# Two attention stages with a new order of steps on every engine, double buffers for probabilities and queries, the fp16 copy on GpSimd and the row normalisation on ScalarE

## The reference

```python
x = x + tanh(g_xattn[0]) * L0_xattn(layernorm(x), ctx, ...)   # q, k, v with bias, then an MLP 256-512-256
x = x + tanh(g_ffn[0])   * L0_ffn(layernorm(x), ...)          # 4-bit blocks, 704 wide
x = x + tanh(g_xattn[1]) * L1_xattn(layernorm(x), ctx, ...)   # masked, then @ Wo
x = x + tanh(g_ffn[1])   * L1_ffn(layernorm(x), ...)          # top 2 of 8 experts

# the core of both attentions, 16 heads of 16
q = (x @ Wq + bq).reshape(B, N, 16, 16)
scores = einsum('bnhd,bmhd->bhnm', q, k) * scale
attn = softmax(scores, axis=-1)
out = einsum('bhnm,bmhd->bnhd', attn, v).reshape(B, N, 256)
```

## Time and profile before

| | us |
|---|---|
| median of 3 runs | 799.55 |
| lowest, highest | 798.21, 802.42 |
| the profiled execution | 796.8 |
| its span | 795.0 |

### The profile page before, as it was taken

The page is one execution under the profiler, slowest core; times in us unless marked ns, Lnnn a source line. Parts: engine busy times, 40 slices in busy tenths (PEclk is TensorE's granted clock), DMA queues, the critical chain, the costliest instruction groups (busy, mean ns, idle before and its releaser), DMA issues.

```text
span 795.0 us, 16679 instructions
## 1 busy us (share of the span) xinstructions
PE 606.7 (76%) x5555; PEld 534.3 (67%) x5555; DVE 565.0 (71%) x1205; ACT 368.3 (46%) x905; POOL 205.8 (26%) x185
## 2 busy tenths in 40 slices
PE   4547787879934588888896599999874599999960
PEld 3237677769933377777785488888764389999950
DVE  5956766757898689999985367878747695455437
ACT  2335656563214444444443246565635355555530
POOL 3434243350020000000001133342500366555530
PEclk9999999999975599999998799999965599999995
DMA  7010000003000000000000000000059212222219
GB/s 219 1 60 1 2 2 2 2 2 110 0 1 0 0 1 0 0 0 0 0 1 1 0 2 2 2 2 2 2 177 381 73 48 80 75 81 78 77 50 307
DMA packets 27626, 36.62 MB, mean 46 GB/s; under 512 B 4024, under 2 KB 22265, under 8 KB 27438
## 3 DMA queue, kind: packets, MB, share of 16 engines
q1 hardware_dynamic: 23822, 25.56, 9.9%
q0 software_dynamic: 3744, 10.23, 4.2%
HBM read 26.47 MB, written 9.31 MB: 45 GB/s over the span
## 4 chain that ended last, share of the span: by engine, by line
PE 33%; DVE 22%; issue 6%; ACT 2%; DMA 1%; DVEq 1%; POOL 0%; SPq 0%; ACTq 0%; POOLq 0%
PE ps L1358 8%; PE ps L1359 7%; PE ps L1360 7%; PE ps L1459 3%; PE ps L1742 2%; DVE fhs L696 2%; DVE fh L754 2%; DVE x_sb L940 2%; DVE fha L705 1%; DVE fha L704 1%; PE ps L1684 1%; PE ps L1428 1%; DVE el_w L817 1%; PE ps L1678 1%; PE ps L1719 1%
## 5 line engine op out<-in xcount | busy, mean ns | idle before, releaser
L989 POOL TENSOR_TENSOR p_lo<-prob,p_hi 128x616 f16<-128x616 f32 x64 | 87.4, 1365 | 165.9 <-ACT prob L1100 162.4
L970 POOL TENSOR_TENSOR rstd<-mv,eps_col 128x16 f32<-128x16 f32 (+2 forms) x6 | 1.3, 209 | 272.7 <-DVE mv L471 272.7
L1108 ACT ACTIVATE pT<-ps 128x512 f32<-128x512 f32 (+1 forms) x96 | 50.7, 533 | 40.8 <-PE ps L1444 40.7
L577 DVE TENSOR_REDUCE smax<-ps 128x8 f32<-128x616 f32 x64 | 50.8, 794 | 19.0 <-PE ps L1360 12.8
L582 DVE TENSOR_TENSOR prob<-ps,smax 128x308 f32<-128x308 f32 x128 | 55.3, 474 | 7.3 <-POOL p_lo L989 3.0
L1358 PE MATMUL ps<-kbd_hi,q_hi 128*128 128x308 f32 x128 | 50.7, 396 | 10.7 <-DVE q_lo L566 9.3
L1032 POOL DMA_INDIRECT y_rows<-rn,dst_row x39 | 43.1, 1106 | 54.6 <-DVE rn L919 53.4
L460 DVE CAST ehT_hi<-ehid 128x512 fp32r<-128x512 f32 x39 | 16.7, 428 | 52.9 <-ACT ehid L1335 52.9
L1459 PE MATMUL ps<-vbd_flat,pT 128*128 128x34 bf16 (+1 forms) x1600 | 47.2, 183 | 6.0 <-ACT pT L1108 4.7
L1028 POOL DMA_INDIRECT xin<-x_rows,src_row x39 | 38.2, 979 | 52.5 <-DVE dst_row L886 40.9
L1099 ACT ACTIVATE p_hi<-prob 128x616 f16<-128x616 f32 x64 | 46.9, 733 | 9.6 <-DVE prob L582 9.4
(11 more groups left out here) (280 smaller groups left out, 2034.1 us busy)
## 6 DMA issues: line engine op xcount, KB each, us to landing
el_w<-in_L_ffn_W_dram SPq DMA_DIRECT2D x16, 512.0 KB, 9.8
eh_w<-y_rows SPq DMA_DIRECT2D x16, 256.0 KB, 6.2
x_sb<-in_x_dram SPq DMA_DIRECT2D x4, 512.0 KB, 8.6
x_rows<-rn SPq DMA_DIRECT2D x4, 512.0 KB, 10.0
out_dram<-x_sb SPq DMA_DIRECT2D x16, 128.0 KB, 4.5
stage<-in_L_xattn_W_dram SPq DMA_DIRECT2D x2, 512.0 KB, 3.7
eb<-in_L_ffn_b_dram SPq DMA_DIRECT2D x1, 1024.0 KB, 9.4
w<-in_L_ffn_w_down_dram SPq DMA_DIRECT2D x1, 704.0 KB, 7.6
```

Of the source, the lines that this page charges most:

```text
L577: ch.link(dve.tensor_reduce(top.rearrange("p (b h) -> p b h", h=HPB), sc, AX.X, ALU.max))
L989: pool.tensor_tensor(p_lo[:, c], prob[:, c], p_hi[:, c], ALU.subtract).then_inc(s["lo"], 1)
L1108: act.activation(dst, ps[:, 4 + g % 2, 0:(c[g + 1] - c[g]) * P // 2], ACT.Copy).then_inc(s["pev"], 1)
```

## The change

- `normalise` moves from VectorE to ScalarE, as an activation with scale `rstd` and bias `shift_a` = -mean x rstd. GpSimd makes `shift_a` (`shift_rows`, two small operations) before the barrier in front of each attention.
- `exp` is done once, in single precision, in place. `p_hi` is now a copy with conversion on GpSimd (`high_half`), followed by the difference (`low_half`), in the order low(t-1, second half), high(t, first), low(t, first), high(t, second).
- `prob`, `p_hi`, `p_lo`, `q_hi`, `q_lo` have two buffers, by the parity of the tile or pair.
- Each engine's `step(k)` gives every operation a distance in tiles. TensorE: query of k+2, x transposes of k+3, o transposes of k-2, scores of k+1, p transposes 1 and 2 of k-1, project of k-2, values of k-1, p transpose 0 of k. VectorE: residual of k-3, xT_lo of k+2, shift and norm, o_low of k-2, moments of k-3, q_lo of k+2. ScalarE: normalise k+4, first exponential, copies, xT_hi of k+3, q_hi of k+2, second exponential last. All steps are written out, and no engine has a loop in these stages.

The core of the diff:

```diff
-                def exp(t, h):
-                    if h == 0:
-                        att_wait(act, n, "lo", 2 * t)
-                        att_wait(act, n, "pt", 3 * t)
+                def exp(t, par, h):
                     att_wait(act, n, "shifted", 2 * t + h + 1)
                     c = slice(h * HM // 2, (h + 1) * HM // 2)
-                    act.activation(p_hi[:, c], prob[:, c], ACT.Exp).then_inc(s["hi"], 1)
-                    act.activation(prob[:, c], prob[:, c], ACT.Exp).then_inc(s["exp"], 1)
+                    act.activation(prob[:, par, c], prob[:, par, c], ACT.Exp).then_inc(s["exp"], 1)
...
+                def normalise(p):
+                    att_wait(act, n, "xt", p)
+                    for k in range(2):
+                        t = 2 * p + k
+                        ins = act.activation(xn[:, k], x_sb[:, t], ACT.Identity, bias=shift_a[:, n, bass.ds(t, 1)],
+                                             scale=rstd[:, 2 * n, bass.ds(t, 1)])
+                    ins.then_inc(s["xn"], 1)
...
+            def shift_rows(k, n, part):
+                pool.wait_ge(rs[n], part)
+                ch.link(pool.tensor_tensor(shift_a[:, k], mv[:, n, :, 0], rstd[:, n], ALU.mult))
+                pool.tensor_scalar(shift_a[:, k], shift_a[:, k], -1.0, None, ALU.mult).then_inc(rs[n], 1)
...
+            def high_half(n, t, h):
+                att_wait(pool, n, "exp", 2 * t + h + 1)
+                if h == 0:
+                    att_wait(pool, n, "pt", 3 * (t - 1))
+                c = slice(h * HM // 2, (h + 1) * HM // 2)
+                pool.tensor_copy(p_hi[:, t % 2, c], prob[:, t % 2, c]).then_inc(s["hi"], 1)
+            def both_halves(n):
+                for t in range(TILES):
+                    if t:
+                        low_half(n, t - 1, 1)
+                    high_half(n, t, 0)
+                    low_half(n, t, 0)
+                    high_half(n, t, 1)
+                low_half(n, TILES - 1, 1)
...
-                    att_wait(dve, n, "lo", 2 * (t - 1) + h + 1)
+                    att_wait(dve, n, "lo", 2 * (t - 2) + h + 1)
...
-                    att_wait(act, n, "scores", 4 * p)
+                    att_wait(act, n, "scores", 4 * (p - 1))
```

The new step of TensorE and of ScalarE:

```diff
+                def step(k):
+                    t, soon, now = k, k + 3, k + 2
+                    if 0 <= now < TILES and now % 2 == 0:
+                        query(now // 2)
+                    if 0 <= soon < TILES and soon % 2 == 0:
+                        x_transpose(soon // 2)
+                    if 0 <= t - 2 < TILES:
+                        o_transpose(t - 2)
+                    if 0 <= t + 1 < TILES:
+                        scores(t + 1, 0)
+                    if 0 <= t - 1 < TILES:
+                        p_transpose(t - 1, 1)
+                        p_transpose(t - 1, 2)
+                    if 0 <= t - 2 < TILES and n:
+                        project(t - 2)
+                    if 0 <= t + 1 < TILES:
+                        scores(t + 1, 1)
+                    if 0 <= t - 1 < TILES:
+                        values(t - 1)
+                    if 0 <= t < TILES:
+                        p_transpose(t, 0)
...
+                def step(k):
+                    t, later, soon, now = k, k + 4, k + 3, k + 2
+                    if 0 <= later < TILES and later % 2 == 0:
+                        normalise(later // 2)
+                    if 0 <= t < TILES:
+                        exp(t, t % 2, 0)
+                    if 0 <= t - 1 < TILES:
+                        p_out(t - 1, 0)
+                    if 0 <= soon < TILES and soon % 2 == 0:
+                        x_high(soon // 2)
+                    if 0 <= t - 2 < TILES:
+                        o_high(t - 2)
+                    if 0 <= now < TILES and now % 2 == 0:
+                        q_high(now // 2, now // 2 % 2)
+                    if 0 <= t - 1 < TILES:
+                        p_out(t - 1, 1)
+                        p_out(t - 1, 2)
+                    if 0 <= t < TILES:
+                        exp(t, t % 2, 1)
```

186 lines of the change are left out of this document (59 added, 127 removed).

## The result

| | before | after |
|---|---|---|
| median, us | 798.88 | 753.68 |
| lowest, highest | 798.06, 802.42 | 752.68, 754.52 |
| the profiled execution | 796.8 | 754.5 |
| its span | 795.0 | 752.8 |

The ratio of the medians is 0.9426, with a 95% interval of 0.9394 to 0.9457: 45 us faster, where 34 were forecast. The time lies 3.3 us under the lower end of the range.

What follows compares the result with a forecast made beforehand. TensorE was taken to bound both attentions. Gains of 7.7 + 19.1 - 2.2 in the first and 4.7 + 7.3 - 2.5 in the second made 34 us, off the median 799.55: 765.5, forecast 766 us, range 757 to 779.

Steps and rivals of the forecast that it cites:

- rival A: Both attentions: TensorE is the bound, 758 to 772 us with the forecast's pair prices; chance 0.62.
- floor 11.1 plus 0.5 for hand-overs without slack: First attention: a pair takes 11.6 us, TensorE's summed steps of 11.1 plus 0.5; bounds 11.1 to 12.8.
- a flat 0.4: Second attention: 0.4 us taken off TensorE's busy 14.13 per pair, giving a floor of 13.7.
- 476.3 or so: Second attention's start: GpSimd's difference of tile 3 starts at 476.3 us, before at 480.96; gain 4.7.
- That pace is half clock: Both attention starts: TensorE runs at half clock up to the scores of tile 1.
- rival C: Clock: the two starts stay at half clock two steps longer, 5 us each way, 771 to 776 or 761; chance 0.08.
- 77.0: First attention's start: GpSimd's difference of tile 3 starts at 77.0 us, before at 84.70; gain 7.7.
- 10.3 given: First attention's end: about 10.3 us from the tile 15 mark, before 8.15; loss 2.2.
- code that is written out where four engines had loops: Both attentions: written-out code costed at nothing; the loops' register work goes, code loading grows by little.
- B: Chain exponential, GpSimd copy, p_hi transposes becomes the bound; copy 1.04 us, pairs 12.6 and 14.3, total 774; chance 0.20.
- D: Tiles t and t+1 don't overlap since some buffer still ties them; only xn and q_lo won, 783 us; chance 0.05.
- E: GpSimd paces each tile with two copies and two differences; 34 us slower, about 833; chance 0.05.

Runs made afterwards that it cites:

- the matmuls in the gaps: The changed kernel plus extra never-read TensorE matmuls in its waits at each attention's start and last three steps: 749.21 us, ratio 0.9350 to the kernel before.
- The experiment with the longer copy: The changed kernel plus a second, never-read GpSimd copy of 308 columns ahead of each copy to p_hi: 759.98 us, ratio 0.9487 to the kernel before.

## Why the prediction was off by 12 us

The mechanism of rival A, the forecast, was right: TensorE is the bound in both attentions, the waits of the earlier trace rows are gone and the clock stays at 1.00 between 80 and 148. Several terms were mis-sized, mostly in the same direction; the largest are the prices of a pair.

**The pair prices.** The step that failed is "floor 11.1 plus 0.5 for hand-overs without slack", which gave 11.6, and 14.0 for the second "(13.7 to 14.6)". Measured 10.96 and 13.39, both under the floors that were the lower bounds. Six pairs of each give 64.7 against 68.2 and 79.5 against 82.5: 6.5 us of the miss. The 0.5 was the larger error: the hand-over without slack costs 0.07 in each tile, 0.14 in a pair. The floor erred in the p_lo transposes, taken as 0.54 and 0.26 and measured at 0.46 and 0.20 (98.54, 99.00, 99.20 above), 0.28 per pair; the query erred the other way (1.52 where 1.42 was taken) and the o transposes with the rest took back about as much. For the second attention a flat 0.4 was taken off the busy time of 14.13; 0.7 was in it; no run takes that 0.7 apart.

**The starts.** For the second attention "476.3 or so" (its terms add up to 476.6), shifted by the 26.9 us that the stage now starts earlier (GpSimd's last operation ahead of it ends at 415.07, before at 442.00), is 449.4, and 445.2 came: 4.2 us of the miss. The step that failed is "That pace is half clock", taken from the earlier trace rows and applied "up to the scores of tile 1". The granted clock was at 0.50 from 416 to 422 us and at 1.00 from 424 on, ahead of all scores, so that the first p_hi transposes started at 431.4, where the sum has 435.3. This is rival C in its better direction, which had 5 us. To tile 3 of the first attention 77.0 was given and 76.7 came, by luck: the half pace ended at 60.7 us, so that the p_hi transposes of tile 0 came 1.5 us ahead of the sum (63.5 for 65.0), and the two steps behind them took 1.2 us more than it had. No run was made in which only a start changed its clock; the matmuls in the gaps left the second attention's start as it was.

**The ends.** 141.41 to 150.40 is 9.0 against 10.3 given (8.15 before): 1.3 us in favour. The second attention's end took 524.64 to 540.67, 16.0 us; before it was 12.6 and 2.5 more had been given, so 0.9 against. That end has a granted clock of 0.57 from 528 to 532 us.

**What had no term.** The gap between the stages grew by 2.8 us (180.12 to 442.0 before, 150.40 to 415.07 after). In the profile of after the MLP starts at half clock for some 6 us, which as an estimate is 3 us; with the gaps filled the clock stays up and the gap is 261.3 us, 0.6 under that of before. The other kernels show that this start falls either way, so it is as much the execution that was profiled as the change. What follows the second attention is 0.5 longer. To cost "code that is written out where four engines had loops" at nothing was wrong too: it is 6 us (and three engines had loops, TensorE's steps were written out), though the sum had most of this gain inside the pair, since the floor knows no loops. What it shows is that 6 of the 45 us would have come without any new order.

The sum: 6.5 + 4.2 + 0.3 + 1.3 - 0.9 - 2.8 - 0.5 is 8.1 us of profile time, and with the forecast's 34 it makes the 42.2 of the spans within rounding. The other 3 of the 45 lie between profiles and medians: the profile of before is 2.1 under its median and that of after 0.8 over, which the sum could not know.

**The rivals.** B: the copy is 697 ns in the mean of 64, against 0.70 forecast and 0.63 to 1.04 as bounds:

```profile
L978 POOL TENSOR_TENSOR p_lo<-prob,p_hi 128x616 f16<-128x616 f32 x64 | 87.2, 1362 | 5.1
L972 POOL CAST p_hi<-prob 128x616 f16<-128x616 f32 x64 | 44.6, 697 | 68.5 <-ACT prob L1101 68.5
```

The experiment with the longer copy shows that B was a real rival: with 0.52 us more, 0.36 per tile come through, so at 1.04 the first attention would have lost some 4 us, by estimate from these two. The Trainium skill, "GPSIMD Engine Reference", Performance versus the Vector engine, gives 1.8 cycles per element as the best case of a tight loop, from which the prediction had its estimate of 0.92 us; the 64 copies do not bear it out. The same section also has 1.03 cycles for the shortest loops, which as an estimate is 0.53 us here. The copies of 616 and of 308 columns (0.697 and 0.441 us) differ by 0.83 ns per element, close to that figure, and leave about 0.19 us that does not grow with the size. D falls: tiles t and t+1 overlap. E falls: GpSimd is busy 8.14 of 10.96.

**What the prediction did not see.** It listed waits and removed them one by one. The runs show that they are not additive: the new buffers and the moved operations alone give 12 us, the query chain's distance on top of them makes it 10 us slower, the whole order gives 28. The new order on the old single buffers was not tried.
